# The last pair's lower row tile normalised and stored on its own, ahead of the last product's additions

## What is computed

```
x = _layernorm(x + _L0_attn_ref(x), axis=-1)
x = _layernorm(x + _L0_xattn_ref(ctx_4096, ctx_4096, x), axis=-1)
x = _layernorm(x + _L0_ffn_ref(x, W_base, gate_W, A, B), axis=-1)

def _layernorm(x, axis=-1, eps=1e-05):
    m = jnp.mean(x, axis=axis, keepdims=True)
    v = jnp.var(x, axis=axis, keepdims=True)
    return (x - m) / jnp.sqrt(v + eps)
```

## Time and profile before

| | us |
|---|---|
| median of 3 runs | 1966.44 (1965.95 to 1971.0) |
| the profiled execution, its own time | 1964.43 |
| its span in the trace | 1962.6 |
| outside the span | 1.83 |

### The profile page before, as it was taken

How to read it: one execution, slowest core, us unless ns; L and a number is a source line. 1 busy time by engine, 2 the same in 40 slices (tenths; PEclk the granted TensorE clock), 3 DMA queues, 4 the chain that set the end, 5 groups by cost and what they waited for, 6 DMA issues and landing times. The chain is left out here.

```text
span 1962.6 us, 27015 instructions
## 1 busy us (share of the span) xinstructions
PE 1779.3 (91%) x10194; PEld 953.8 (49%) x10210; DVE 1361.5 (69%) x2605; ACT 791.6 (40%) x939; POOL 200.1 (10%) x358
## 2 busy tenths in 40 slices
PE   3989999999853959999999999998899999999997
PEld 2656665767531425445544445443344444444443
DVE  3878888888859866777666777799654655565463
ACT  5888888788745211222222212133231222213111
POOL 1223232323200000000000000000010010010000
PEclk9999999999975989999999999999999999999998
DMA  8899999999758499999999999945999879988882
GB/s 279 196 278 269 287 249 288 269 282 257 223 199 239 113 240 254 269 255 236 247 256 266 250 227 227 231 164 161 294 259 253 274 221 259 266 249 252 248 242 108
DMA packets 565563, 472.70 MB, mean 241 GB/s; under 512 B 498416, under 2 KB 502512, under 8 KB 544624
## 3 DMA queue, kind: packets, MB, share of 16 engines
q1 hardware_dynamic: 565424, 470.87, 87.8%
HBM read 237.51 MB, written 109.58 MB: 177 GB/s over the span
## 5 line engine op out<-in xcount | busy, mean ns | idle before, releaser
L1558 PE MATMUL bank_f<-w_hi_f,a_cols_f 128*128 128x512 f16 x3584 | 1090.4, 381 | 78.0 <-DVE w_lo_f L1292 36.4
L1558 PE MATMUL bank_f<-w_lo_f,a_cols_f 128*128 128x512 f16 x1792 | 683.6, 381 | 0.0
L1558 PEld LDWEIGHTS bank_f<-w_hi_f,a_cols_f 128*128 128x128 f16 x3584 | 352.2, 98 | 507.4 <-DMA a_cols_f<-rows_f 41.7
L1148 ACT ACTIVATE rows_f<-xn_f 128x1024 f16<-128x1024 f32 x78 | 82.4, 1057 | 500.1 <-DMA xn_f<-x_scratch 337.8
L1558 PEld LDWEIGHTS bank_f<-w_lo_f,a_cols_f 128*128 128x128 f16 x1792 | 176.0, 98 | 204.0 <-issue 3.2
L1323 DVE SCALAR_TENSOR_TENSOR y_f<-bank_f,w_iscale_f,y_f 128x512 f32<-128x512 f32 x192 | 134.5, 742 | 169.3 <-PE bank_f L1558 169.2
L649 PE MATMUL ps_s_fast<-k_both_fast,q_hi_fast 128*128 128x256 f16 x1024 | 170.8, 275 | 7.4 <-DMA k_both_fast<-v_lo_fast 6.4
L1284 DVE TENSOR_TENSOR rows_f<-xn_f,rows_f 128x1024 f16<-128x1024 f32 x78 | 94.3, 1209 | 97.6 <-ACT rows_f L1148 97.6
L1323 DVE SCALAR_TENSOR_TENSOR y_f<-bank_f,w_iscale,y_f 128x512 f32<-128x512 f32 x192 | 134.7, 743 | 34.8 <-PE bank_f L1558 31.6
L1284 DVE TENSOR_TENSOR rows_f<-sums_f,rows_f 128x1024 f16<-128x1024 f32 x63 | 76.8, 1219 | 114.8 <-ACT rows_f L1148 114.6
L1148 ACT ACTIVATE rows_f<-sums_f 128x1024 f16<-128x1024 f32 x63 | 66.3, 1052 | 195.9 <-DMA a_cols_f<-rows_f 193.3
(11 more groups left out here) (210 smaller groups left out, 2300.8 us busy)
## 6 DMA issues: line engine op xcount, KB each, us to landing
xbuf_fast<-x SPq DMA_DIRECT2D x32, 1024.0 KB, 7.8
x_scratch<-x2buf_fast SPq DMA_DIRECT2D x32, 1024.0 KB, 5.7
y_f<-x_scratch SPq DMA_DIRECT2D x32, 1024.0 KB, 7.8
xn_f<-x_scratch SPq DMA_DIRECT2D x62, 512.0 KB, 4.9
kept_scratch<-a_cols_f SPq DMA_DIRECT2D x45, 512.0 KB, 3.4
xn<-x_scratch SPq DMA_DIRECT2D x45, 512.0 KB, 6.8
a_cols_f<-kept_scratch SPq DMA_DIRECT2D x45, 512.0 KB, 8.7
cbuf<-ctx_in SPq DMA_DIRECT2D x16, 1024.0 KB, 5.9
```

The lines of the kernel that those rows point to most:

```text
L1148: nc.scalar.activation(rows[g % 2][:, 0], source(i), ACT.Copy).then_inc(a_hi, 1)
L1558: ins = nc.tensor.matmul(bank[i][:], a_cols[:, i, part + kk, :], ww[:, W_SLOT[i], kk, :], start=(kk == 0 and part == 0 and ww is w_hi), st ...
```

## The change

It concerns only the end of the last slot. The lower row tile (t = 1) of the last pair is aggregated by DVE before the last product's two additions, then scaled by POOL (one column instead of two), normalised by ACT and stored. The upper tile follows behind the additions in the same four steps. The two BN_AGGR, four POOL steps and two 1 MB stores become: one BN_AGGR ahead and one behind, with one more linked memset and one more settling memset; twice four POOL steps on one column; the four ACTIVATEs in the order lower first half, lower second half, upper first half, upper second half; and four stores of 512 KB. For all other slots `norm` does the same four steps as before, with its two waits in the other order.

```diff
+        def last_tiles(s):
+
+            return [slice(1, 2), slice(0, 1)] if s == SLOTS - 1 else [slice(0, 2)]
...
-                store_out(SLOTS - 1)
                 for i in range(2):
-                    sp.wait_ge(y_stored[i], 16 * (SLOTS // 2))
-                sp.wait_ge(first_stored, 16 * NP_)
+                    t = 1 - i
+                    for c, data, stored in ((0, y_first, first_stored), (1, y[(SLOTS - 1) % 2][:], y_stored[(SLOTS - 1) % 2])):
+                        sp.wait_ge(normalised, 2 * (NP_ - 1) + 2 * i + c + 1)
+                        sp.dma_start(rows_out(SLOTS - 1, c)[:, t], data[:, t]).then_inc(stored, 16)
+                for i in range(2):
+                    sp.wait_ge(y_stored[i], 16 * (SLOTS // 2 + i))
+                sp.wait_ge(first_stored, 16 * (NP_ + 1))
...
-                    pool.wait_ge(mv_ready, n + 1)
                     after(pool, normalised, 2 * n)
-                    g.tensor_tensor(var_eps[:], mv[:, :, 1], columns[:, EPS_AT], ALU.add)
-                    chain.link(g.tensor_tensor(nmean[:], mv[:, :, 0], columns[:, MINUS_ONE], ALU.mult))
-                    chain.link(g.tensor_tensor(rs[:], var_eps[:], columns[:, MINUS_HALF], ALU.pow))
-                    g.tensor_tensor(nb_[:], nmean[:], rs[:], ALU.mult).then_inc(ln_ready, 1)
+                    for i, tiles in enumerate(last_tiles(s)):
+                        pool.wait_ge(mv_ready, n + 1 + i)
+                        g.tensor_tensor(var_eps[:, tiles], mv[:, tiles, 1], columns[:, EPS_AT, tiles], ALU.add)
+                        chain.link(g.tensor_tensor(nmean[:, tiles], mv[:, tiles, 0], columns[:, MINUS_ONE, tiles], ALU.mult))
+                        chain.link(g.tensor_tensor(rs[:, tiles], var_eps[:, tiles], columns[:, MINUS_HALF, tiles], ALU.pow))
+                        g.tensor_tensor(nb_[:, tiles], nmean[:, tiles], rs[:, tiles], ALU.mult).then_inc(ln_ready, 1)
...
-                normalise(SLOTS - 1)
+                for i in range(2):
+                    act.wait_ge(ln_ready, NP_ + i)
+                    t = 1 - i
+                    for data in (y_first, y[(SLOTS - 1) % 2][:]):
+                        nc.scalar.activation(data[:, t], data[:, t], ACT.Identity, bias=nb_[:, t:t + 1], scale=rs[:, t:t + 1]).then_inc(normalised, 1)
...
+                chain.link(v.memset(tmp[:], 0.0))
+                after(dve, ln_ready, NP_ - 1)
+                chain.settle()
+                v.bn_aggr(mv[:, 1], stats[:, 1].rearrange("p a b c -> p (a b c)")).then_inc(mv_ready, 1)
                 update(SLOTS - 1, 12, 13)
-                aggregate(SLOTS - 1)
+                chain.link(block_stats(SLOTS - 1, C12))
+                chain.link(block_stats(SLOTS - 1, C11))
+                chain.settle()
+                v.bn_aggr(mv[:, 0], stats[:, 0].rearrange("p a b c -> p (a b c)")).then_inc(mv_ready, 1)
```

## The result

The changed kernel takes 1965.41 us in the median of 22 runs (1961.68 to 1970.73), the kernel before 1969.61 in 22 runs of its own, the three shown ahead of the prediction among them (1965.04 to 1971.54). The ratio is 0.9983 with a 95% interval of 0.9976 to 0.999: a gain of 0.17%, 3.3 us, small but clear of the noise of that many runs. In microseconds the interval reaches from 2.0 to 4.7. The two medians lie 4.2 apart, the two means 3.5. The forecast was a gain of 3.6, and 1962.8 with a range of 1960.5 to 1966.0. The time lies in the range, near its upper end, because the median of before itself stood 3.2 higher with 22 runs than with three.

The account below looks back on a forecast made before the run. PE, busy 91%, sets the time overall, but a 14.65 us chain follows its last matmul. Issuing 2.20 earlier and landing 1.40 faster shorten the span by 3.6: 1966.44 - 3.6 = 1962.8 us, range 1960.5 to 1966.0.

Parts of the forecast that it names:

- The mechanism and its sum: Kernel's end: lower tile finished and stored beside the last additions, smaller stores landing sooner; span 3.6 us shorter.
- The last issue: SP at the kernel's end: last store issued at 1955.78 instead of 1957.98, 2.20 us earlier.
- landing: Last 512 KB store lands 2.77 us after its issue, where the last 1 MB store took 4.17.
- from landing to the end: Time between the last store's landing and the span's end, taken over from the kernel before: 0.45 us.
- DVE's insertion: Memsets and one aggregate ahead of the last product's additions on DVE: first addition 0.31 us late.
- the aggregate of the upper tile: DVE's remaining aggregate behind the last additions and statistics: ends at 1952.01 instead of 1951.81, 0.20 us late.
- The stores in turn: Slower rival: each of the last four stores begins only when the previous has landed; 1968.4 us, chance 0.04.
- the step on what can be told apart: Whole kernel: a measurement tells about 0.3%, 5.9 us, from no change; 3.6 is 0.18%, so "same" has 0.93.
- Elsewhere: Other 15 slots of the second half: two waits ahead of POOL's steps change places, costing nothing; no PE instruction moves.
- The level: Forecast median of the whole kernel: 1966.44, the median of three runs before, less 3.6, gives 1962.8 us.
- the held POOL: Rival: DVE work holds the lower tile's POOL steps by the full 2.70 us; median 1964.8, chance 0.07.
- 2.20 and 1.40: Gains at the kernel's end: last store issued 2.20 us earlier, and landing 1.40 us sooner after its issue.

Follow-up runs that it names:

- splitting run: Kernel before with only the last pair's two 1 MB stores split into four of 512 KB; last matmul's end to span's end 13.47 us, a gain of 1.18.
- earlier work alone: The change with two 1 MB stores, each behind the upper tile's ACTIVATE of its half; last matmul's end to span's end 13.50 us.
- stores at the end: The change with all four 512 KB stores waiting for the last ACTIVATE; last matmul's end to span's end 14.58 us.
- doubled insertion: The change with linked memset, settling memset and aggregate ahead of DVE's last additions done twice; last matmul's end to span's end 11.24 us.

## Why the prediction was right or wrong

- **The mechanism and its sum were right.** 3.6 were forecast, the tail shrank by 3.75 and the timed runs by 0.17%. The last issue was forecast 1955.78 - 1947.95 = 7.83 behind the last matmul and came at 7.74; landing 2.77, measured 2.73; from landing to the end 0.45, measured 1963.3 - 1962.87 = 0.43. These are the missing 0.15.
- **DVE's insertion** was 0.32 (forecast 0.31, though the two terms behind it, 0.13 and 0.17, add to 0.30). But the aggregate of the upper tile ended only 0.15 later instead of 0.20: the first addition behind the insertion took 0.68 and released the next one after 0.59, where it was 0.73 and 0.66 before. This term was mis-sized by 0.05.
- **POOL** took 1.23 for the lower tile and 1.22 for the upper (forecast 1.26), and was not held; the rows that the prediction gave for this were the right ones: the hold is real but needs another kind of neighbour.
- **The stores in turn** were given 0.04 and are out by two runs. The rule of the Trainium skill, page "DMA: Bandwidth & Descriptors", section "Bandwidth", to send 1 MB or more at once does not decide here: the four stores of the splitting run kept the DMA engines at a share of 0.99 or more, and it gained 1.18.
- **What failed is the step on what can be told apart.** The prediction put 0.93 on "same" because 3.6 us is under the 0.3% that it said a measurement of this kernel can tell. For three runs that lie 5 us apart this was a fair bound. With 22 on each side the interval is 0.07% wide to either side and the shift of 0.17% is beyond it. The forecast in microseconds was therefore of a gain that was measured as a gain, while the chances named it no change. The bound should have been worked out from the number of runs instead of taken as fixed.
- **Elsewhere** was put at nothing. In the slot ahead of the last one, where the kernels differ by the order of POOL's two waits, POOL starts 0.15 behind its aggregate's end, where it was 0.08 before, and ACT starts 0.07 later with it. It costs nothing, since DVE and PE keep their distance there.
- **The level** was 2.6 too low: 1962.8 against 1965.41. The term at fault is the starting point, 1966.44, the median of only three executions of a kernel that scatters over 6.5 us; more runs moved it to 1969.61, and the 4.2 between the medians, instead of 3.6, took 0.6 of that back. That 1965.41 still fell into the range was in part luck: the upper end came from the held POOL, which did not happen, and an allowance of 1.2 for scatter. The prediction's remark that the profiled execution stood 2.0 below the median was a sign of this and was used only for the lower end of the range.
- **Read but not priced:** that the two halves of the change are worth little alone. The prediction's 2.20 and 1.40 add up rightly for both together, but neither is what its half is worth alone: the split alone gives 1.18 and the earlier work alone 1.15, because either way all 5.09 of bytes follow the first send of the tail. From the first issue, 0.85 + 5.09 + 0.50 + 0.45 = 6.89 remain: that gives 14.65 before, 13.52 for the split alone, 13.49 for the whole stores and 14.62 for the stores at the end, each within 0.05 of its measured tail. In the change it would give 10.68; the first two stores are through before the third starts (a share of 0.39 from 1959.50 to 1960.00), and the upper tile's issues set the end at 10.90.

## What to carry to other kernels

At the end of a kernel look for the moment at which the first of the last bytes leaves, not only for the last issue: the tail is that moment plus all bytes that still have to go, or the last issue plus its own landing, whichever is later (each with the fixed times ahead of the first byte and behind the last). Making results ready earlier pays only when they are also sent earlier, and splitting stores pays only when the pieces are ready at different times. When a change touches only a short stretch, measure from a fixed event at that stretch's start; here the last matmul's end scattered by 4.7 us over the traces, and the tail of the change came out the same twice.

## What the runs showed of the hardware that was not expected

- A store from SBUF to DRAM in an otherwise empty queue landed in 2.6 to 2.7 for 512 KB, while the 512 KB stores of the kernel's busy part never did under 3.1; the first bytes follow the issue after about 0.85.
- An addition directly behind a small settled instruction ran in 0.68 instead of 0.73 and let the next one start 0.07 earlier. It is seen in each run that has the insertion right ahead of the addition (the change twice, the whole stores, the stores at the end, the doubled insertion); why is open.
- DVE normalised two pieces of 128x512 in 1.00 in all, ACT the same amount in 1.52:

```profile
1953.96 1.52 ACT L1279 ACTIVATE cbuf<-cbuf,nb_f,rs_f 128x512 f32<-128x512 f32 x2 [1.96 <-POOL nb_f L1142]
1953.96 1.00 DVE L1562 TENSOR_SCALAR y_f<-y_f,rs_f,nb_f 128x512 f32<-128x512 f32 x2 [1.34 <-POOL nb_f L1142]
```
